# A two-layer graph kernel: more gathers beside the linear attention, sums kept in PSUM banks, a split clear, and eight expert slots

## The reference, cut to what matters

```python
xn = _layernorm(x)
x = x + gnn_l0(xn) + mix_l0(xn)          # 8 heads of 32; linear attention
x = x + experts_l0(_layernorm(x))        # 8 experts with a capacity
xn = _layernorm(x)
x = x + gnn_l1(xn) + mix_l1(xn)          # two graph attentions: 4 heads of 128, then 1 of 256
x = x + experts_l1(_layernorm(x))        # 32 experts, hidden 64

# the graph attention, the same form three times
ex    = exp(alpha - amax[dst])
attn  = ex / segment_sum(ex, dst)[dst]
out   = segment_sum(h[src] * attn[..., None], dst)
```

## Time and profile before

| | us |
|---|---|
| median of 3 runs | 3194.65 (3193.55 to 3198.88) |
| the profiled execution, its own time | 3198.91 |
| the span in its trace | 3197.3 |
| stages: linear attention / score / sum of layer 0 | 165 / 435 / 278 |
| sum with 4 heads / with 1 head / experts of layer 1 | 442 / 403 / 146 |
| busy, of the span: PE / PEld | 2147.4 (67%) / 1473.6 (46%) |
| busy, of the span: DVE / ACT / POOL | 2060.7 (64%) / 1246.2 (39%) / 1712.0 (54%) |

### The profile page before, as it was taken

How to read it: one execution, slowest core, us unless ns; L and a number is a source line. 1 busy time by engine, 2 the same in 40 slices (tenths; PEclk the granted TensorE clock), 3 DMA queues, 4 the chain that set the end, 5 groups by cost and what they waited for, 6 DMA issues and landing times. The chain is left out here.

```text
span 3197.3 us, 48907 instructions
## 1 busy us (share of the span) xinstructions
PE 2147.4 (67%) x10992; PEld 1473.6 (46%) x10993; DVE 2060.7 (64%) x3850; ACT 1246.2 (39%) x3616; POOL 1712.0 (54%) x1802
## 2 busy tenths in 40 slices
PE   3634777767998479948674599997763566665262
PEld 2322333335555345634564477776652344444141
DVE  7586877778788443353478588888593556666332
ACT  2323333325776312124200476765400566663010
POOL 1586777742555211141554777775467777770324
PEclk9866888868999589978776799999856899985597
...
GB/s 141 200 182 229 264 263 261 260 244 137 216 218 196 80 234 260 279 123 121 352 396 236 224 280 274 282 271 221 180 341 195 151 148 148 149 148 15 98 194 151
DMA packets 456713, 668.49 MB, mean 209 GB/s; under 512 B 67154, under 2 KB 334092, under 8 KB 456001
## 3 DMA queue, kind: packets, MB, share of 16 engines
...
...
HBM read 491.69 MB, written 176.23 MB: 209 GB/s over the span
## 5 line engine op out<-in xcount | busy, mean ns | idle before, releaser
L1533 POOL DMA_INDIRECT xn<-table,src_col x572 | 587.4, 1027 | 180.6 <-issue 150.1
L1574 PE MATMUL sum_h_ps<-xn,sum_h_hot 128*128 128x261 f32 (+1 forms) x1936 | 525.4, 414 | 188.1 <-DVE xn L1588 145.8
L1574 PEld LDWEIGHTS sum_h_ps<-xn,sum_h_hot 128*128 128x128 f32 x1936 | 367.8, 200 | 338.4 <-DVE xn L1588 243.9
L1092 POOL DMA_INDIRECT arena_a<-table,src_col x264 | 265.3, 1005 | 269.9 <-issue 188.7
L978 POOL DMA_INDIRECT arena_b<-table,src_col x336 | 318.5, 948 | 111.7 <-issue 110.2
L1588 DVE TENSOR_TENSOR xn<-xn,al 128x514 f32<-128x514 f32 (+1 forms) x352 | 243.8, 693 | 160.9 <-DMA xn<-table,src_col 157.0
L1597 DVE TENSOR_TENSOR arena_a<-arena_a,sum_h_ps 128x522 f32 (+1 forms) x440 | 246.3, 560 | 61.8 <-issue 43.3
L1707 PE MATMUL sum_ps<-xn,sum_hot 128*128 128x264 f32 x880 | 245.1, 405 | 31.9 <-DVE arena_a L1730 12.8
L1690 POOL TENSOR_TENSOR xn<-xn,al 128x264 f32<-128x264 f32 x220 | 158.1, 720 | 168.7 <-DMA xn<-edge_h 166.0
L1009 ACT ACTIVATE xn<-score_ps_en 128x512 f32<-128x512 f32 x220 | 131.4, 597 | 293.4 <-PE score_ps_en L995 292.8
L999 PE MATMUL score_ps_hd<-arena_a,score_hot 128*128 x1320 | 239.5, 331 | 0.0
...
## 6 DMA issues: line engine op xcount, KB each, us to landing
xn<-edge_h SPq DMA_DIRECT2D x220, 264.0 KB, 3.1
...
xn_t<-edge_rows SPq DMA_DIRECT2D x110, 256.0 KB, 4.6
score_h_hot<-hots SPq DMA_DIRECT2D x220, 128.0 KB, 13.2
...
```

Of the source, the lines that this page charges most:

```text
L1092: pool.indirect_dma_start(rows[:, q, s, :], None, table, bass.IndirectOffsetOnAxis(ap=K.src_col[:, w * SUB + s:w * SUB + s + 1], axis=0)). ...
L1533: pool.indirect_dma_start(rows[w][:, s, 0:RW], None, table, bass.IndirectOffsetOnAxis(ap=K.src_col[:, w * SUB + s:w * SUB + s + 1], axis=0 ...
L1574: ins = pe.matmul(ps[:, u, b, 0:part], lhsT=hot[:, w % QH, s, :], rhs=rows[w][:, s, b * part:(b + 1) * part], start=(s == 0), stop=(s == S ...
```

## The change

`EARLY0` goes from 26 to 30, and `early_terms` gets a third home for the terms, at the end of `K.xn`. In the linear attention VectorE's subtraction of the mean and its multiplication by the reciprocal spread are each cut into five instructions of one tile.

In the sum of layer 0 the tile's sum is no longer collected in `acc` by VectorE: TensorE adds all windows of one destination tile in one PSUM bank (`start=False`), tile t in bank t mod 8. For that it reads, once for four windows, four bank numbers and four counts that say how many banks must have been freed, both from the new table `K.bank`. ScalarE waits for the last window of each tile (`K.tile_end`), copies the bank to `acc` and clears it. VectorE makes all one-hots, as two instructions, and the message of both halves as one. GpSimd has no work there.

In both sums of layer 1 ScalarE clears 13 tiles of `acc` and VectorE the other 12, each by an arithmetic instruction. In the experts of layer 1 the ring has 8 slots and rows are loaded 5 tiles ahead. The tables are made in the items stage.

```diff
-EARLY0 = 26
+BANKS = 8
+EARLY0 = 30
...
+def load_four(engine, values, low, high):
+
+    return engine.bass.values_load_multi_w_load_instructions(values, engines=(engine.engine,), min_val=low, max_val=high)[1]
...
             step(dve.tensor_copy(K.window[:, :], t_f[:, :]))
+            step(dve.tensor_scalar(K.bank[:, 0, :], K.window[:, :], 1, None, ALU.add))
+            step(dve.tensor_scalar(K.bank[:, 1, :], K.window[:, :], BANKS - 1, None, ALU.bitwise_and))
+            step(dve.tensor_copy(key_i[:, :], key_t[:, :]))
+            step(dve.tensor_scalar(K.tile_end[:, 0:NT - 1], key_i[:, :], EB.bit_length() - 1, None, ALU.logical_shift_right))
+            step(dve.memset(K.tile_end[:, NT - 1:NT], W))
...
-    return K.al[:, WS * H0:WS * H0 + fits * n], K.arena_a[:, far:far + (EARLY0 - fits) * n]
+    more = (K.arena_a.shape[1] - far) // n
+    free = NT * D - (EARLY0 - fits - more) * n
+    return (K.al[:, WS * H0:WS * H0 + fits * n], K.arena_a[:, far:far + more * n],
+            K.xn[:, :, :].rearrange("p t d -> p (t d)")[:, free:])
...
-                dve.tensor_tensor(part, part, gmean[:, :].unsqueeze(2).broadcast_to([P, groups, MD]), ALU.subtract).then_inc(s_cen, 1)
+                near_c = kv[:, c * U:(c + 1) * U, :].rearrange("p t (g d) -> p t g d", d=MD)
+                for t in range(U):
+                    mean_t = gmean[:, t * 2 * MH:(t + 1) * 2 * MH].unsqueeze(2).broadcast_to([P, 2 * MH, MD])
+                    ins = dve.tensor_tensor(near_c[:, t], near_c[:, t], mean_t, ALU.subtract)
+                ins.then_inc(s_cen, 1)
...
-                step(dve.tensor_tensor(part, part, grstd[:, :].unsqueeze(2).broadcast_to([P, groups, MD]), ALU.mult))
+                for t in range(U):
+                    rstd_t = grstd[:, t * 2 * MH:(t + 1) * 2 * MH].unsqueeze(2).broadcast_to([P, 2 * MH, MD])
+                    ins = dve.tensor_tensor(near_c[:, t], near_c[:, t], rstd_t, ALU.mult)
+                step(ins)
...
+            none = K.eps[:, 0:1].unsqueeze(2).broadcast_to([P, half, acc.shape[2]])
+            act.activation(acc[:, 0:half, :], none, ACT.Copy, scale=0.0).then_inc(s_clear, 1)
...
-            dve.memset(acc, 0.0).then_inc(s_acc, 1)
+            same = K.eps[:, 0:1].unsqueeze(2).broadcast_to([P, NT - half, acc.shape[2]])
+            dve.tensor_tensor(acc[:, half:, :], same, same, ALU.subtract).then_inc(s_acc, 1)
             message(0, 0)
             message(0, 1)
+            dve.wait_ge(s_clear, 1)
...
+            act.wait_ge(s_none, 1)
+            for t in range(NT):
+                end = act.value_load(K.tile_end[0:1, t:t + 1], min_val=1, max_val=W)
+                act.wait_ge(s_sum, end + Q)
+                act.activation(acc[:, t, :], ps[:, t % BANKS, 0:ROW0], ACT.Copy).then_inc(s_out, 1)
+                act.wait_ge(s_out, t + 1)
+                if t + BANKS < NT:
+                    act.activation(ps[:, t % BANKS, 0:ROW0], none[:, :], ACT.Copy).then_inc(s_free, 1)
...
+            pe.wait_ge(s_none, 1)
+            for u in range(BANKS):
+                ins = pe.matmul(ps[:, u, 0:ROW0], lhsT=K.ident[:, :], rhs=none[:, :], start=True, stop=True)
+            ins.then_inc(s_free, BANKS)
...
-                    w, q, u = i * J + j, j % Q, j % U2
-                    if j in made:
-                        pe.wait_ge(s_hot, i * len(by_act) + made[j] + 3)
-                    else:
-                        pe.wait_ge(s_hot2, i * len(by_dve) + by_dve.index(j) + 1)
-                    pe.wait_ge(s_msg0, w + 1)
-                    pe.wait_ge(s_msg1, w + 1)
-                    pe.wait_ge(s_acc, w + 1)
+                    w, q = i * J + j, j % Q
+                    if j % 4 == 0:
+                        needs = load_four(pe, K.bank[0:1, 0, bass.ds(w, 4)], 1, NT)
+                        banks = load_four(pe, K.bank[0:1, 1, bass.ds(w, 4)], 0, BANKS - 1)
+                    pe.wait_ge(s_hot, w + 1)
+                    pe.wait_ge(s_msg, w + 1)
+                    pe.wait_ge(s_free, needs[j % 4])
                     for s in range(SUB):
-                        ins = pe.matmul(ps[:, u, 0:ROW0], lhsT=hot[:, q, s, :], rhs=rows[:, q, s, :], start=(s == 0), stop=(s == SUB - 1))
+                        ins = pe.matmul(ps[:, bass.ds(banks[j % 4], 1), 0:ROW0].rearrange("p a c -> p (a c)"), lhsT=hot[:, q, s, :], rhs=rows[:, q, s, :],
+                                        start=False, stop=(s == SUB - 1), skip_group_check=True)
                     ins.then_inc(s_sum, 1)
...
+                dve.wait_ge(s_sum, w + 1)
+                for s in range(SUB):
+                    ins = dve.tensor_scalar(hot[:, q, s, :], K.iota_row[:, :], K.rel_col[:, bass.ds(w * SUB + s, 1)], None, ALU.is_equal)
+                ins.then_inc(s_hot, 1)
                 dve.wait_ge(s_rows[q], 16 * (i * (J // Q) + j // Q + 1))
-                view = rows[:, q, 0, :].rearrange("p (h r) -> p h r", h=H)
-                dve.tensor_tensor(view, view, al[:, bass.ds(w * SUB, 1), :].rearrange("p s h -> p (s h)").unsqueeze(2).broadcast_to([P, H, R]),
-                                  ALU.mult).then_inc(s_msg0, 1)
-
-            def one_hot(i, j):
-                w = i * J + j
-                dve.wait_ge(s_sum, w + 1)
-                dve.tensor_tensor(hot[:, j % Q, :, :], K.rel_col[:, bass.ds(w * SUB, SUB)].unsqueeze(2).broadcast_to([P, SUB, P]),
-                                  K.iota_row[:, :].unsqueeze(1).broadcast_to([P, SUB, P]), ALU.is_equal).then_inc(s_hot2, 1)
-
-            def add(i, j):
-                w, u = i * J + j, j % U2
-                window = dve.value_load(K.window[0:1, bass.ds(w, 1)], min_val=0, max_val=NT - 1)
-                dve.wait_ge(s_sum, w + 1 + Q)
-                dve.wait_ge(s_acc, w + U2)
-                dve.tensor_tensor(acc[:, window, :], acc[:, window, :], ps[:, u, 0:ROW0], ALU.add).then_inc(s_acc, 1)
-
-            dve.sem_inc(s_acc, U2)
-            dve.memset(one[:, :], 1.0).then_inc(s_one, 1)
-            dve.memset(acc, 0.0).then_inc(s_zero, 1)
-            dve.wait_ge(s_zero, 1)
-            for j in range(AHEAD):
-                message(0, j)
-            with aligned(dve, 0, turns - 1) as i:
+                view = rows[:, q, :, :].rearrange("p s (h r) -> p s h r", h=H)
+                dve.tensor_tensor(view, view, al[:, bass.ds(w * SUB, SUB), :].unsqueeze(3).broadcast_to([P, SUB, H, R]),
+                                  ALU.mult).then_inc(s_msg, 1)
...
-        Q, U2 = 4, 2
+        Q, U2, AHEAD = 8, 2, 5
...
-            load(0, 0)
-            load(0, 1)
+            for q in range(AHEAD):
+                load(0, q)
```

78 lines of the change are left out of this document (19 added, 59 removed).

## The result

The changed kernel takes 3115.83 us (median of 4 runs, 3113.22 to 3118.84) against 3194.88 us (4 runs, 3193.55 to 3198.88): a ratio of 0.9751, with a 95% interval of 0.9734 to 0.9768, or 79 us less. The forecast was 3144.1, 50.5 us less, in a range of 3100 to 3186. The profiled execution after has a span of 3117.2 us, before 3197.3, so the two traces differ by 80.1 us.

What follows compares the result with a forecast made beforehand. The kernel was taken as a sum of 17 barrier-separated stages, each with its own bound. Terms of -1, -20.1, +8, -3, -35 and +0.6 made -50.5 us, from the median 3194.65 to 3144.1, range 3100 to 3186.

Steps and rivals of the forecast that it cites:

- Gathers moved: Linear attention takes 30 groups for 26, its long VectorE instructions cut: -1 us there, -20.1 us in the score stage.
- Sum of layer 0: Layer 0's softmax-weighted sum: TensorE's sequencer sets the pace with its register loads and checks, +8 us (-3 to +97).
- Rival (c): Layer 0's sum: a load of four costs four loads, 1.21 us; +89 us, kernel 3233, slower than before; chance 0.09.
- Rival (a): Layer 0's sum: range checks after the first cost little, 35 us less, VectorE's 1.03 to 1.08 us paces, total 3109; chance 0.20.
- Two of the signs named: Layer 0's sum: near 286 us (250 or 330 if register prices are wrong), TensorE's idle time put to its own issue.
- Clearing: Layer 1's sums: splitting the clearing between VectorE and ScalarE frees the first gather with four heads; -3 us (-6 to +3).
- Experts: Layer 1's experts: eight slots and a lead of five bring a tile from 2.35 to 1.7 us; -35 us (-47 to -19).
- With eight the ring no longer binds: Layer 1's experts: the ring of four sets 2.35 us a tile; with eight, TensorE or the transfers come next.
- Tables: Items stage: five small VectorE operations (1.3 us) ahead of a wait with 0.80 us of room; +0.6 us.

Runs made afterwards that it cites:

- e2: Changed kernel with VectorE's 2560-element instructions whole again (linear attention 182.2 us), experts' rows loaded 2 tiles ahead (129.5), layer 1 sums cleared by two memsets.
- e3: Changed kernel with 26 gather groups (linear attention 160.7 us, score 435.3), experts' ring of 4 with lead 3 (159.0), layer 1 sums cleared by one memset.
- e1: Changed kernel with the four bank numbers TensorE loads per four windows in layer 0's sum left unchecked: 3083.19 us, ratio 0.9642, that stage 231.8 us.
- e4: Changed kernel with one of VectorE's two one-hots per window left out (layer 0 sum 267.9 us) and half of each expert's weights loaded (experts 98.9).
- f2: e1 with one of two one-hots left out (layer 0 sum 206.3 us), experts' lead of 3 (113.9), VectorE's 12 tiles cleared by memset (four heads 429.7).
- g1: g2 with, at four heads, VectorE's wait for the first gathered rows moved ahead of its first one-hot: 3069.27 us, ratio 0.9615, stage 430.2.
- g2: e1 with VectorE's 12 tiles of layer 1's sums cleared by memset, the wait behind the first one-hot: 3075.79 us, ratio 0.9619, four-head stage 436.2.

## Why the prediction was right, and where it was off

**The direction, the range and most of the places were right.** Five of seven terms came within 1.5 us, three of them by luck, as told below. The gain was 80.1 us in the traces and not 50.5; 18.3 of the missing 29.6 lie in the sum of layer 0, 10.1 in the experts, and 2.6 in stages that nothing touched.

**Gathers moved** (-20.1 and -1; measured -19.4 and +0.5). The price of 1.25 us a gather held. Of the 25.5 us lost to long instructions before, 9.4 were still lost after, where I left 3.5: in each round the addition of 1280 elements and the first of each five short ones still hold a gather, for 1.3 to 1.7 us. GpSimd ended at 262.3 and not 257. That the stage is only 0.5 us longer is luck: GpSimd's drain, which had ended the stage before, fell off the path, 3 us that I had not foreseen. e2 and e3 show both halves of the trade by themselves.

**Sum of layer 0** (+8; measured -10.3). The step was right that named TensorE's sequencer as the pace (e1, e4), and that VectorE's 1.03 us came next (1.01 in e1), then TensorE's 0.89 us (f2). The size was off. The terms of the prediction make 4.76 + 2 x 0.10 = 4.96 us for four windows, and they took 4.61: 19 us over 55 groups. The load of four took 0.33 us, not 0.40: 7.7 us. A window's own register sum, wait and address took 0.33 us, not 0.38: some 10 us. The rest is in the checks and gaps. The 0.40 stood on 32 ns, a register operation, for each register after the first; it was 10 ns (332 against 302). The rule of the Trainium skill ("Runtime: NRT & Kernel Launch", section "Instruction fetch mechanics"), some 200 ns for each register, would have given 0.8 us. The page states it for loads over uncached AXI; the table here lies in SBUF, and the 332 ns of the trace speak against the rule for this load. The costs beyond the first value are in the checks, 164 ns each, that the row did show. Rival (c), four loads' price, is out by the same row. Rival (a), cheap checks, is out too: 146 ns is their median over all. But its result, a pace of 1.03 us, is what e1 made. Two of the signs named did not show: the stage took 268 us, between the 286 of the forecast and the 250 of rival (a), and TensorE's idle time was put down to VectorE and not to its own issue, until e4 took VectorE's work away.

**Clearing** (-3; measured -3.1). The agreement is luck: -3.7 and +0.6 both lie within the 6 us by which these stages move from run to run, and the reason was wrong. I took the memset itself for what holds the first gather, as against the rule in the Trainium skill ("SBUF — State Buffer", section "Who interferes with whom"), by which a VectorE instruction with at most one SBUF input does not contend with GpSimd, outside the modes that use both ports. g1 against g2 shows that the rule holds for the memset, and that the tensor_tensor behind it does the holding, one instruction earlier than the trace shows it at work. So the 7.3 us less of hold (13.76 to 6.49) came from VectorE's shorter piece of the clearing, and by this reading a wait moved would have brought as much without any of the new clearing, which no run shows by itself. That gathers go on beside the memset with one head was misread too: the earlier trace rows has the second gather, and the fifth took 2.46 us. The 2560 elements in 2.82 us are 1.10 ns each and not 1.04; the 6.7 us for 6264 came out all the same, at 6.68.

**Experts** (-35; measured -45.1). "With eight the ring no longer binds" held, but the formula behind it, (landing + 2.6 tiles) / 4, took the ring for the whole of the 2.35 us; its 2.6 tiles stand in no row, they are what makes it come out. The lead of two tiles was the larger part: 28.7 of 45.1 us. The two knobs can't be turned one by one either: a lead of one less than the ring is worse than before in both rings (159.0, 173.3). For what comes next I named TensorE at 1.35 to 1.5 us and the transfers at 1.48, and added 0.2 us for crowding, to 1.7; it was 1.53. That allowance is 9.4 of the 10.1 us. Both named bounds were wrong, though their numbers were close: halving the weights' bytes takes off only 1.9 us (e4), TensorE needs 1.10 us, and the 1.53 are ScalarE's queue.

**Tables** (+0.6; measured -0.1): nothing to see.

**The chances.** 0.43 stood on the forecast's own range of 3125 to 3160; the time came out at 3115.8, between it and rival (a)'s 3109, by none of the rivals: two terms of the forecast were each too careful.
